# The fourth attention unit turned by VectorE and a store and load, its context sum moved behind the third output product

## The reference

```python
h_q = (x @ w_q.T).reshape(b, lq, H, DH)
h_k = (key_value_states @ w_k.T).reshape(b, lk, H, DH)
h_v = (key_value_states @ w_v.T).reshape(b, lk, H, DH)
score = jnp.einsum('bqhd,bkhd->bhqk', h_q, h_k) + position_bias[None]
score = jnp.where(m, score, -jnp.inf)
score = jnp.where(m, jax.nn.softmax(score, axis=-1), 0.0)
attn = jnp.einsum('bhqk,bkhd->bqhd', score, h_v).reshape(b, lq, H * DH)
out = attn @ w_out.T
```

## Time and profile before

| | |
|---|---|
| median of 3 runs | 800.29 us (800.02 to 800.35) |
| profiled execution | 800.21 us |
| its span in the profile | 798.4 us |
| TensorE busy | 793.6 us |
| VectorE busy | 633.1 us |
| ScalarE busy | 352.9 us |
| GpSimd busy | 298.5 us |

### The profile page before, as it was taken

How to read it: one execution, slowest core, us unless ns; L and a number is a source line. 1 busy time by engine, 2 the same in 40 slices (tenths; PEclk the granted TensorE clock), 3 DMA queues, 4 the chain that set the end, 5 groups by cost and what they waited for, 6 DMA issues and landing times.

```text
span 798.4 us, 12698 instructions
## 1 busy us (share of the span) xinstructions
PE 793.6 (99%) x4090; PEld 675.5 (85%) x4090; DVE 633.1 (79%) x1066; ACT 352.9 (44%) x949; POOL 298.5 (37%) x279
## 2 busy tenths in 40 slices
PE   9999999999999999999999999999999999999998
PEld 7888888888888888888888888888888888888886
DVE  6877878886893596889988879788877978877775
ACT  6633432432341253554534345343534434446683
POOL 3123021020111032746455446554544654434136
PEclk9999999999999999999999999999999999999999
DMA  8464674575456648627566666656665675653002
GB/s 302 146 200 171 223 247 137 177 256 171 154 183 212 210 160 274 212 68 233 168 216 206 195 183 200 224 153 212 199 213 154 207 225 159 200 195 139 1 1 106
DMA packets 103217, 145.54 MB, mean 182 GB/s; under 512 B 9944, under 2 KB 74584, under 8 KB 97648
## 3 DMA queue, kind: packets, MB, share of 16 engines
q1 hardware_dynamic: 102720, 144.33, 55.7%
q10 hardware_dynamic: 432, 0.39, 0.2%
HBM read 93.31 MB, written 51.38 MB: 181 GB/s over the span
## 4 chain that ended last, share of the span: by engine, by line
PE 98%; DMA 1%; DVE 0%; issue 0%; ACT 0%; SPq 0%; DVEq 0%
PE out L1470 11%; PE out L1472 11%; PE out L1471 11%; PE proj L1470 11%; PE proj L1472 11%; PE proj L1471 10%; PE s L1564 7%; PE o L1591 4%; PE s L1471 4%; PE s L1472 4%; PE s L1470 4%; PE t L1591 3%; PE proj L1667 1%; PE proj L1668 1%; PE t L1619 1%; PE t L1575 1%
## 5 line engine op out<-in xcount | busy, mean ns | idle before, releaser
L872 POOL TENSOR_TENSOR w_stage<-w_stage 128x256 f32<-128x256 f32 x30 | 26.9, 898 | 262.9 <-DMA w_stage<-in_wk 241.4
L896 POOL TENSOR_TENSOR bias_mask<-bias_raw,mask_neg 128x512 f32<-128x512 f32 x64 | 75.3, 1184 | 81.4 <-DVE s L1306 67.4
L1042 ACT ACTIVATE s<-s,neg_max 128x128 f32<-128x128 f32 x208 | 71.5, 349 | 52.5 <-DVE neg_max L1309 52.5
L1470 PE MATMUL out<-wo_hi,o_hi 128*128 128x512 f32 x224 | 88.5, 395 | 0.0
L1472 PE MATMUL out<-wo_lo,o_hi 128*128 128x512 f32 x224 | 87.8, 392 | 0.0
L1471 PE MATMUL out<-wo_hi,o_lo 128*128 128x512 f32 x224 | 87.3, 390 | 0.0
L1470 PE MATMUL proj<-x_hi,w_hi 128*128 128x512 f32 x210 | 85.0, 405 | 0.0
L884 POOL TENSOR_TENSOR w_lo<-w_stage,w_hi 128x512 fp32r<-128x512 f32 (+1 forms) x52 | 59.4, 1155 | 68.1 <-ACT w_hi L988 68.1
L1472 PE MATMUL proj<-x_lo,w_hi 128*128 128x512 f32 x210 | 82.5, 393 | 0.0
L1471 PE MATMUL proj<-x_hi,w_lo 128*128 128x512 f32 x210 | 82.0, 390 | 0.0
L1347 DVE TENSOR_TENSOR acc<-out,acc 128x512 f32<-128x512 f32 x100 | 67.2, 673 | 14.1 <-PE out L1472 14.0
(11 more groups left out here) (370 smaller groups left out, 2123.5 us busy)
## 6 DMA issues: line engine op xcount, KB each, us to landing
k_spill<-ring SPq DMA_DIRECT2D x64, 256.0 KB, 3.4
v_spill<-ring SPq DMA_DIRECT2D x64, 256.0 KB, 2.5
p_turned<-probs SPq DMA_DIRECT2D x208, 64.0 KB, 2.8
probs_t<-p_turned SPq DMA_DIRECT2D x52, 256.0 KB, 2.9
big_stage<-in_wv SPq DMA_DIRECT2D x8, 1024.0 KB, 8.7
w_stage<-in_wq SPq DMA_DIRECT2D x32, 256.0 KB, 3.5
k_first<-k_spill SPq DMA_DIRECT2D x8, 1024.0 KB, 7.3
v_first<-v_spill SPq DMA_DIRECT2D x8, 1024.0 KB, 9.7
```

The lines of the kernel that those rows point to most:

```text
L896: pool.tensor_tensor(bias_mask[:, j % 2], bias_raw[:, i % 2][:, None, :].to_broadcast([P, HALF, P]), mask_neg[:, halves[half], :], ALU.add ...
L1042: last = act.activation(scores_of(j)[:, b], scores_of(j)[:, b], ACT.Exp, bias=neg_max[:, col:col + 1], accum_out=row_sum[:, col:col + 1])
L1470: pe.matmul(to[:], left_hi, right_hi, start=first and n == 0, stop=False, skip_group_check=True)
```

## The change

`BLOCKED` begins at unit 3 in place of unit 4. Unit 3's `T` and `PT` go; its `N` now works in the score's PSUM bank and is followed by `TZ` and `TS`, at the place of its `N`; `TL` stands where `T` stood. Its `PV` moves from before `("S", 5)` to between `normal(5)` and `("OUT", 0, 3)`. `OH` and `OL` go with `PV`. The conditions on `BLOCKED` in all the engines' functions follow.

```diff
-BLOCKED = range(4, 2 * SPLIT)
+BLOCKED = range(3, 2 * SPLIT)
...
-            steps += [("S", 3), *product(first, 4), *prod[2], ("WX", m, 3), ("T", 2), ("EXP", 3), ("BM", 4), *prod[5], ("N", 3),
+            steps += [("S", 3), *product(first, 4), *prod[2], ("WX", m, 3), ("T", 2), ("EXP", 3), ("BM", 4), *prod[5], *normal(3),
                       ("PV", 2), ("WOL", 1), *load]
-            steps += [*prod[7], ("S", 4), *prod[3], ("T", 3), ("EXP", 4), ("BM", 5), ("BL", 4), *prod[4],
+            steps += [*prod[7], ("S", 4), *prod[3], ("TL", 3), ("EXP", 4), ("BM", 5), ("BL", 4), *prod[4],
                       *outs(0, 0), *normal(4), ("KL", 2), *sums, *outs(0, 1)]
...
         if p == 1:
-            steps += [("PV", 3), ("S", j + 1), ("S", j + 2), ("WX", m, 1), ("EXP", j + 1), ("EXP", j + 2), *biased(j), *biased(j + 1),
-                      *biased(j + 2), ("TL", j), *outs(o, 2), *normal(j + 1), *outs(o, 3), *prod[1], *normal(j + 2), *outs(o, 4), *prod[6],
+            steps += [("S", j + 1), ("S", j + 2), ("WX", m, 1), ("EXP", j + 1), ("EXP", j + 2), *biased(j), *biased(j + 1),
+                      *biased(j + 2), ("TL", j), *outs(o, 2), *normal(j + 1), ("PV", 3), *outs(o, 3), *prod[1], *normal(j + 2), *outs(o, 4), *prod[6],
                       ("WX", m, 2), ("WX", m, 3), *load, *outs(o, 5)]
```

## The result

The changed kernel takes 807.74 us (median of 5 runs, 806.84 to 808.60), the kernel before 800.35 us beside it. The ratio is 1.0093, with a 95% interval from 1.0082 to 1.0105: the change costs 7.4 us. The profiled execution took 808.60 us, span 806.8; it is the slowest of the five.

A forecast was written before the change was run, and what follows sets the result against it. TensorE was taken as the bound, busy 793.6 of 798.4 us. The profiled 800.21 us plus a 5.0 us hole before OUT 0 4 plus 1.6 us of clock cost gave 806.8 us, range 803.0 to 808.9.

The forecast's parts named there:

- the sum's own 803.9: Lower end of the forecast sum for the whole kernel: loads landing after 3.0 us and no clock cost, 803.9 us.
- SP's queue decides: In SP's order, unit 3's stores wait for TZ 3 and hold the weights 19 loads back 13 us.
- Through BM 6 and SC 6: On GpSimd, late weights 19 delay the sums, low parts and BM 6, so VectorE's SC 6 starts 2.7 us late.
- OL 3 behind EXP 6 adds to it: OH 3 follows EXP 6 on ScalarE; OL 3 ends at 366.5, so TensorE's OUT 0 4 is 5.0 us late.
- The clock: After TensorE's hole before OUT 0 4 the granted clock falls; cost between 0 and 2.6 us, taken as 1.6.
- The context sum's move by itself: Moving PV 3 alone, without late loads, was claimed to cost 0.2 us as a hole before OUT 0 4.
- the same sum without the late BM 6: Case of early loads at OUT 0 4: OL 3 ends at about 361.8 and the hole costs 0.2 us.
- N 3's multiply: On VectorE, moving N 3 from SBUF to PSUM should bring its multiply nearer 0.70 us than 1.12.
- PV 3's cover of 1.5 us: On TensorE, PV 3's load lands at 356.2, after 2.9 us, and PV 3's turn is 357.7: 1.5 us cover.
- A gain on TensorE: Removing T 3's four transposes gives TensorE 0.44 us, forecast to be used up by S 6's wait for TZ 4.

The follow-up runs named there:

- e1: Changed kernel with unit 3's four stores moved behind the output weights' load and the weights 19 loads in SP's order: 801.56 us, ratio 1.0017.
- e3: Kernel before, with SP waiting for unit 4's maximum before the output weights' and weights 19 loads: 804.62 us, ratio 1.0055.
- e11: Changed kernel, loads still late, with BM 6 moved in front of the sums of weights 19 on GpSimd: 801.88 us, ratio 1.0018.
- e4: Changed kernel with 18 extra, unused 128x128 matmuls in front of OUT 0 4: 805.76 us, ratio 1.0070.
- e7: Changed kernel with the weights 19 loads issued before the output weights' load, both still behind the stores: 805.12 us, ratio 1.0065.
- e2: Kernel before with only PV 3 moved to its new place, T 3 still on TensorE: 801.61 us, ratio 1.0016.
- e8: e1 with GpSimd's low part 0 of weights 19 made to wait for TZ 4: 802.11 us, ratio 1.0024.
- e6: Changed kernel, stores still in front of the loads, with PV 3 back at its old place before S 5: 803.67 us, ratio 1.0041.
- e9: e5 with GpSimd's BM 6 moved from behind the low parts to the sums of weights 19: 799.89 us, ratio 0.9996.
- e5: e1 with PV 3 placed between the scores of units 5 and 6: 801.34 us over 11 runs, ratio 1.0014.

## Why the prediction was right, step by step

The time, the sign and the mechanism were right: 806.8 us forecast, 807.74 measured, inside 803.0 to 808.9 (whose lower end lies below the sum's own 803.9, though the text says that both ends were cut). After the correction by 1.77 us, the profiled steps stand beside the forecast ones like this:

| step | forecast | measured, corrected |
|---|---|---|
| loads of weights 19 issued | 351.0 | 350.9 |
| GpSimd's sums start | 355.9 | 356.2 |
| BM 6 starts | 360.8 | 361.0 |
| SC 6 starts | 362.0 | 362.3 |
| OL 3 starts | 365.8 | 366.05 |
| OUT 0 4 starts | 366.55 | 366.8 |
| clock's cost, to PV 4 | 1.6 | 1.8 |

The last is PV 4's start, 374.57, less before's 365.77, less 1.77, less the 5.25 us of OUT 0 4. The profiled execution less its offset is 806.8 us. That this is the forecast to a tenth is in part luck: at PV 4 the loss was 5.25 + 1.8 = 7.0 us against 6.6 forecast, and the execution ends only 6.6 us behind before's, so 0.4 us came back behind PV 4, where the prediction let nothing come back.

- **SP's queue decides**: right, and shown by e1, which changes nothing but the order of seven issues. e3 shows that the same lateness by another cause does it too.
- **Through BM 6 and SC 6**: right, and shown by e11: with BM 6 out of the way, 5.9 of the 7.4 us are gone although the weights are as late. What is left is not free of them, since they still delay EXP 5 and the small multiply; no run has PV 3 moved, the loads early and BM 6 early, so how much of the last 1.3 us is theirs is not shown.
- **OL 3 behind EXP 6 adds to it**: right. In e3, without the move, OUT 0 4 is 2.8 us late; in the changed kernel 5.25. The two terms can be read off: SC 6 is 362.28 - 359.32 = 2.96 us late, and from SC 6 to OUT 0 4 it is 368.57 - 364.05 = 4.52 us in place of 361.55 - 359.32 = 2.23, that is 2.29 more.
- **The clock**: right in the changed kernel (e4), though which holes trigger it was not foreseeable: that of 2.82 us (e3) did, that of 2.71 us (e7) did not in the profiled run. The 1.6 us were chosen between 0 and 2.6; the profiles show 1.8 here and 2.8 in e3, so that the size came out close is luck.
- **The context sum's move by itself was mis-sized.** The prediction had "the same sum without the late BM 6", with "the hole would cost 0.2 us". e1 and e2 measured 1.4 us. Its OL 3, ending at 361.8, needs SC 6 near 357.3, right behind SC 5. Missing was that ScalarE, no longer held by OH 3, lets GpSimd's low parts run just when VectorE needs a small multiply from SBUF, so TZ 4, and with it S 6, SC 5, SC 6 (358.3, corrected) and OL 3, are about 1 us late. e8 takes the collision away and loses the same at BM 6: in the changed order OUT 0 4 hangs on OL 3, 3.8 us behind SC 6, whatever delays SC 6. In the changed kernel this did not show, since the late loads keep GpSimd idle there: S 6 waited 0.43 us, as forecast.
- **N 3's multiply** was read as dear because it works in SBUF (1.12 us against 0.70). In the profile after, a multiply of the same size in SBUF took 0.69 us (at 343.55, unit 2) while GpSimd stood idle; the 1.12 us of before ran beside GpSimd's sums. The forecast of about 0.70 held (348.81, 0.70 us), the reason is rather the neighbour than the memory.
- **PV 3's cover of 1.5 us** was overstated, though not by enough to matter. In the changed kernel the load took 4.5 us from its issue at 353.97 and not 2.9, so it landed 1.2 us before PV 3 (359.69). It took 4.1 us in e6, and 5.9 us in e7, where TensorE waited 0.24 us for it, all behind the weights in the same queue; in e1, with nothing large ahead, it took 2.6 us.
- **A gain on TensorE** of 0.44 us exists (e9, span 797.6), but only when PV 3, the stores and BM 6 are all placed for it.

Open is the difference between profile and median: the median after lies 0.9 us over the corrected 806.8, although the profiled run was the slowest of its five, and e5's 1 us over its profile. Either the early stages of these programs vary more, or something later does; the single profiles do not tell.

## What to carry to other kernels

When an operation moves from an engine to a store and load, its transfers take a place in an in-order queue, and a store waits for its data there: look at what is queued behind it, and who needs that first, before you count what the engine saves. Follow the delayed load through the other in-order queues too; here the products got their weights in time, and the loss came from an unrelated bias_mask queued behind them. An early release can hurt as well: it brings two engines to a shared resource at the same time.

## What the runs showed of the hardware

- VectorE's multiply of 4 columns with both inputs in SBUF took 0.16 us alone, 1.24 us (e1) and 1.19 us (e2) beside GpSimd's subtraction of 512 columns, and ended with it. VectorE's additions of `bias_mask`, with one input in PSUM, kept their 0.69 us beside a running GpSimd operation (e1, at 358.82).
- After holes of 5.05, 3.44 and 2.82 us (the changed kernel, e6, e3) the granted clock was at 0.50 of 2.4 GHz; after one of 2.71 us (e7) it had stayed at 1.00. What it cost in the first and the third was 1.8 and 2.8 us: the shorter hole cost more, so the price is not set by the hole's length alone.
- A load of 256 KB behind other loads in SP's queue landed after 4.1 to 5.9 us (the turned probabilities in e6, after and e7), and after 2.6 us in e1, where the weights had gone out 13 us earlier.
